# Self attention of a transformer decoder layer: units taken by threes, narrow diagonal blocks merged, max products placed one by one

## What is computed

```python
y = tgt                                   # (2, 2048, 512), 16 heads of 32
yn = _ln(y, dec_n1_s, dec_n1_b)
y = y + _mha(yn, yn, dec_sa_in_w, dec_sa_in_b, dec_sa_out_w, dec_sa_out_b, sb)   # sb: relative bias + causal mask
y = y + _mha(_ln(y, dec_n2_s, dec_n2_b), memory, dec_ca_in_w, dec_ca_in_b, dec_ca_out_w, dec_ca_out_b, cb)
h = _ln(y, dec_n3_s, dec_n3_b)
y = y + (jax.nn.relu(h @ dec_ff1_w.T + dec_ff1_b) @ dec_ff2_w.T + dec_ff2_b)
```

## Time and profile before

| | |
|---|---|
| median of 3 runs | 2791.2 us (2790.24 to 2792.56) |
| the profiled execution | 2795.43 us, its span 2793.4 us |
| mean granted TensorE clock | 0.987 |
| busy TensorE (PE), weight loads (PEld) | 2702.4 us (97%), 1791.0 us |
| busy VectorE (DVE), ScalarE (ACT) | 1583.1 us (57%), 1262.0 us (45%) |
| stage of self attention | from 396.8 us to 1600 us of the span |

### The profile page before, as it was taken

How to read it: one execution, slowest core, us unless ns; L and a number is a source line. 1 busy time by engine, 2 the same in 40 slices (tenths; PEclk the granted TensorE clock), 3 DMA queues, 4 the chain that set the end, 5 groups by cost and what they waited for, 6 DMA issues and landing times. The chain is left out here.

```text
span 2793.4 us, 40069 instructions
## 1 busy us (share of the span) xinstructions
PE 2702.4 (97%) x12704; PEld 1791.0 (64%) x12704; DVE 1583.1 (57%) x3827; ACT 1262.0 (45%) x2656; POOL 417.2 (15%) x497
## 2 busy tenths in 40 slices
PE   7999989999999999999999899999999999999998
PEld 6788854444444444444444378767778888888886
DVE  5554367777777777777777377567643222222211
ACT  2322113555555555555555545588833322332231
POOL 5000021000000000000000332188556000000000
PEclk9999988999999999999999999999999999999999
DMA  7656663222222222222222398555431000000000
GB/s 223 214 194 200 197 163 83 69 67 69 69 69 70 70 71 69 61 63 60 56 58 54 90 243 259 197 176 182 149 114 50 16 31 31 30 0 30 31 16 15
DMA packets 138950, 272.96 MB, mean 98 GB/s; under 512 B 24886, under 2 KB 56118, under 8 KB 133499
## 3 DMA queue, kind: packets, MB, share of 16 engines
q1 hardware_dynamic: 133530, 255.14, 31.7%
q0 software_dynamic: 5216, 15.33, 1.8%
HBM read 176.02 MB, written 99.98 MB: 99 GB/s over the span
## 5 line engine op out<-in xcount | busy, mean ns | idle before, releaser
L1302 ACT ACTIVATE sa_pr<-sa_st 128x512 f32<-128x512 f32 (+3 forms) x1280 | 611.0, 532 | 536.8 <-DVE sa_st L1365 293.8
L1268 PE MATMUL sa_ov<-sa_pr,sa_v 128*33 128x512 f32 (+3 forms) x2560 | 535.0, 539 | 0.0
L1349 DVE TENSOR_REDUCE sa_part<-sa_mp 128x1 f32<-128x512 f32 x760 | 408.3, 583 | 115.1 <-PE sa_mp L1247 114.3
L1257 PE MATMUL sa_st<-sa_q,sa_k 97*128 97x512 f32 (+3 forms) x1280 | 441.4, 413 | 17.9 <-ACT sa_pr L1302 13.5
L1257 PEld LDWEIGHTS sa_st<-sa_q,sa_k 97*128 97x128 f32 x1280 | 216.3, 189 | 319.7 <-ACT sa_pr L1302 213.0
L1247 PE MATMUL sa_mp<-sa_k,sa_q 96*128 96x512 f32 (+1 forms) x1256 | 362.0, 382 | 10.3 <-PEq L1229 5.3
L1346 DVE CUSTOM_DVE_ANT_0 sa_mp<-sa_mp,sa_ub 128x512 f32<-128x512 f32 (+1 forms) x496 | 308.4, 665 | 77.0 <-PE sa_mp L1247 72.9
L149 PE MATMUL ff_f<-sa_q,ff_w 128*128 128x512 f32 x1024 | 337.2, 390 | 3.1 <-PEq L2068 3.1
L2063 PE MATMUL ff_o<-ff_w,ca_q 128*128 128x512 f32 x1280 | 330.0, 392 | 3.7 <-DVE ca_q L2114 3.7
L2114 DVE TENSOR_TENSOR ca_q<-ca_v,ca_q 128x512 fp32r<-128x512 f32 x128 | 97.5, 762 | 379.3 <-ACT ca_q L2098 379.3
L1268 PEld LDWEIGHTS sa_ov<-sa_pr,sa_v 128*33 128x33 f32 x2560 | 122.0, 110 | 256.2 <-issue 206.6
(11 more groups left out here) (240 smaller groups left out, 3276.7 us busy)
## 6 DMA issues: line engine op xcount, KB each, us to landing
sa_q<-scratch_q SPq DMA_DIRECT2D x96, 256.0 KB, 7.7
sa_k<-scratch_k SPq DMA_DIRECT2D x96, 256.0 KB, 8.9
scratch_q<-sao_qst SPq DMA_DIRECT2D x32, 512.0 KB, 6.6
ca_q<-scratch_q SPq DMA_DIRECT2D x32, 512.0 KB, 4.6
scratch_q<-sa_q SPq DMA_DIRECT2D x28, 512.0 KB, 8.1
scratch_k<-sa_q SPq DMA_DIRECT2D x28, 512.0 KB, 5.3
sa_v<-scratch_v SPq DMA_DIRECT2D x16, 528.0 KB, 13.0
scratch_o<-sa_osb SPq DMA_DIRECT2D x128, 66.0 KB
```

The costliest lines, as they stand in the source:

```text
L1257: pe.matmul(st[bank(u, h)][:, 0:w], ks[n.par][:, h, kb * P:(kb + 1) * P], qs[n.par][:, h, g * GW + c0:(g + 1) * GW], start=True, stop=True ...
L1268: last = pe.matmul(ov[64 * h:64 * h + VW, c0:GW], vs[n.par][:, kb, h, :], pr[:, u % 4, h, 0:GW - c0], start=(u in opens), stop=(u in ends))
L1302: act.activation(pr[:, u % 4, h, 0:w], st[bank(u, h)][:, 0:w], ACT.Exp, scale=SCALE).then_inc(s["exp"], 1)
L1349: dve.tensor_reduce(to, tile, AX_X, ALU.max).then_inc(s["red"], 1)
```

## The change

What it does:

- **Merged blocks.** In each group the block that covers 128 columns and the block that covers 384 share one score tile of 512 columns for each head (unit "P", two matmuls into one tile), and the block that covers 256 columns holds both heads in one tile (unit "J"). "D" is the full-width diagonal block, "B" the last block before the diagonal, "F" any earlier one. Four units of eight tiles become three units of five tiles; a slot has 36 units and 68 tiles for ScalarE instead of 40 and 80. The matmuls are the same.
- **Batches of three** units (13 in a slot instead of 20, a few of them with two). `sa_pr` has six places instead of four.
- **Single max products.** A max product of one head is the smallest piece; four PSUM tiles of one bank take the place of two of two banks. Tables say how many go before each score tile (`MAX_BEFORE`, TensorE) and how many maxima before each bias addition (`REDUCED_BEFORE`, VectorE). The first product of the next slot stands at the start of batch 4 (counted from 0).
- **Opening tables** of its own for slot 0, with 10 products ahead of the first score instead of 4.
- **SyncE's order** in a usual slot: `store(n,0)`, `row(n,2)`, `load(n+1)`, `row(n,3)`, `store(n,1)`, `store(n,2)`, `row(n+1,0)`, `row(n+1,1)`, `store(n,3)`. The load gets one more DMA, 128 columns of the bias table that are there twice now. Slot 0 issues its load first.
- The sums and their inverses move into a buffer of cross attention that is idle at that time.

```diff
-SELF_ORDER = ((0, 2, 3, 1),
...
-STEPS_FROM = 12
...
+SELF_ORDER = ('DPJ', 'FFPFDJB', 'FFFFFBFJPFD', 'FFFFFJFFBFFDFFP')
+BATCHES = ((3,), (3, 2, 2), (3, 3, 3, 2), (3, 3, 3, 3, 3))
+SLOTS = 6
+MAX_FROM = 4
+OPENING_MAX = 35
+MAX_BEFORE = ((1, 0, 3, 1, 1, 1, 0), (1, 2, 0, 2, 1), (0, 0, 3, 1), (0, 1, 1, 0, 0, 0, 1), (2, 1, 2, 0, 2, 1, 1),
...
+REDUCED_BEFORE = ((6, 0, 1), (3, 0, 3), (0, 1, 0, 3), (3,), (9, 0, 0), (7, 0, 0, 1), (5, 0, 0), (7,), (8, 0),
...
+            elif kind == "P":
+                tiles = both(3 * P, 0, (d + 3, 3 * P, 0), (d + 1, P, P))
             else:
+                tiles = [Tile([Part(h, d + 2, 2 * P, 2 * P * h) for h in range(2)], 2 * P, P)]
...
-        tb = [k.sb(f"{name}_tb{i}", [P, 2, 2 * P]) for i in range(2)]
+        tb = [k.sb(f"{name}_tb{i}", [P, 2, 3 * P]) for i in range(2)]
-        pr = k.sb(f"{name}_pr", [P, 4, 2, GW])
+        pr = k.sb(f"{name}_pr", [P, SLOTS, 2, GW])
-        mp = [k.ps(f"{name}_mp{i}", [P, 2, GW]) for i in range(2)]
+        mp = [k.ps(f"{name}_mp{i}", [P, GW]) for i in range(NMB)]
...
             def slot(n, left):
...
+                else:
+                    store(n, 0)
+                    if left == 0:
+                        store_inverses()
+                    row(n, 2)
+                    if left >= 1:
+                        load(n + 1)
+                    row(n, 3)
+                    store(n, 1)
+                    if left == 0:
+                        load_second()
+                    store(n, 2)
+                    if left >= 1:
+                        row(n + 1, 0)
+                    if left >= 1:
+                        row(n + 1, 1)
+                    store(n, 3)
...
+            def max_product(n, x):
+                if x == 0:
                     landed(pe, n, "in", 6)
...
+                waits(pe, s["exp"], NTL * n + emptied(i) + 2)
+                for h, kb, c0, at in tile.parts:
+                    last = pe.matmul(st[i % NST][:, at:at + GW - c0], ks[n.par][:, h, kb * P:(kb + 1) * P],
+                                     qs[n.par][:, h, g * GW + c0:(g + 1) * GW], start=True, stop=True)
+                last.then_inc(s["scores"], 1)
...
             def slot(n, left):
-                for u in range(0, NU, 2):
-                    if isinstance(n.n, int) and n.n == 0 and u == 0:
+                for j in range(NJ):
+                    if is_first(n) and j == 0:
                         pe.wait_ge(s["init"], inits)
-                    ahead = list(after(n, u, left))
-                    for i in range(2):
-                        if ahead:
-                            scores(*ahead[i])
-                        for m, a in steps_at(n, u + i, left):
-                            max_step(m, a)
-                    values(n, u)
-                    values(n, u + 1)
+                    for maxima, ahead in places(n, left, (opening if is_first(n) else usual)[j], following(n, j, left)):
+                        for m, x in maxima:
+                            max_product(m, x)
+                        for m, i in ahead:
+                            scores(m, i)
+                    for u in batches[j]:
+                        values(n, u)
```

More of the change, by code:

```diff
@@ L930, in self_units @@
+OPENING_REDUCED_BEFORE = ((9, 0, 1), (5, 0, 2), (4, 0, 3, 0), (12,), (10, 2, 0), (9, 0, 0, 0), (8, 0, 1), (9,),
+                          (9, 1), (7, 0, 1), (5, 0, 3), (6, 0, 0), (0, 0, 4, 0, 0, 2))
+INVERSE_AT = 1
+Unit = namedtuple("Unit", "group tiles")
+Tile = namedtuple("Tile", "parts biased table")
+Part = namedtuple("Part", "head block first at")
 def self_units():
+    both = lambda biased, table, *blocks: [Tile([Part(h, *x) for x in blocks], biased, table) for h in range(2)]
     out = []
@@ L941, in self_units, with self_batches @@
+        assert next(far, None) is None and sum(BATCHES[g]) == len(order)
+    return out
+def self_batches():
+    out, u = [], 0
+    for size in itertools.chain(*BATCHES):
+        out.append(range(u, u + size))
+        u += size
     return out
@@ L1049, in self_attention @@
     N = NPAIR * B
[L1050 to L1058, removed]
@@ L1059, in self_attention @@
-    NCH = 1 + max(m[3] for m in msteps if m is not TURN)
-    usual, opening = self_steps_at(NU, NM)
+    units, batches, products = self_units(), self_batches(), self_max_products()
+    NU, NJ, NX = len(units), len(batches), len(products)
+    opens = [min(u for u in range(NU) if units[u].group == g) for g in range(GB)]
+    ends = {max(u for u in range(NU) if units[u].group == g): g for g in range(GB)}
+    tiles = [(u, t) for u in range(NU) for t in units[u].tiles]
+    tiles_of = [[i for i, (v, _) in enumerate(tiles) if v == u] for u in range(NU)]
@@ new lines, in self_attention @@
+    near = [i for i, (_, t) in enumerate(tiles) if t.biased]
+    NTL, NB = len(tiles), len(near)
+    turns = [x for x in range(NX) if products[x] is TURN]
+    heads_of_max = [x for x in range(NX) if x not in turns]
+    late = next(x for x in heads_of_max if products[x][0] >= KB // 2)
+    last_of = [max(x for x in heads_of_max if products[x][0] // TT == g) for g in range(GB)]
+    NCH = 1 + max(products[x][3] for x in heads_of_max)
+    begun = sum(sum(MAX_BEFORE[j]) for j in range(MAX_FROM, NJ))
@@ L1064, in self_attention, with emptied @@
     ROW = (3 * HD, 3 * HD)
[L1066 to L1086, removed]
+    def emptied(i):
+        return i - NST if i >= NST else max(e for e in range(NTL) if e % NST == i) - NTL
@@ new lines, in following, with places, is_first, width @@
+    def following(n, j, left):
+        if j + 1 < NJ:
+            return [(n, i) for u in batches[j + 1] for i in tiles_of[u]]
+        return [(n + 1, i) for u in batches[0] for i in tiles_of[u]] if left else []
+    def places(n, left, places_of, ahead):
+        for i, places_here in enumerate(places_of):
+            yield [(n + d if d else n, x) for d, x in places_here if left >= d], ahead[i:i + 1]
+    def is_first(n):
+        return isinstance(n.n, int) and n.n == 0
+    def width(i):
+        return sum(GW - p.first for p in tiles[i][1].parts)
```

299 lines of the change are left out of this document (154 added, 145 removed), and 3 rows, old and new, of the table SELF_ORDER.

## The result

| | before | after |
|---|---|---|
| median | 2791.2 us (2790.24 to 2795.99) | **2775.0 us** (2773.57 to 2782.22) |
| ratio | | 0.9943, 95% interval 0.9927 to 0.9958 |
| the profiled execution | 2795.43 us, span 2793.4 | 2773.57 us, span 2771.5 |
| mean granted TensorE clock | 0.987 | 0.977 |

A forecast was written before the change was run, and what follows sets the result against it. TensorE was taken as the bound, paying about 0.3 us a batch for changing matmul kind, plus waits. Usual slots −3.5, slot 15 −2 and slot 0 −6 made −11.5 off 2791.2: 2780 us, range 2712 to 2812.

The forecast's parts named there:

- The load decides: Usual slots: the load, queued behind store(n,0), lands at about 22.0 us; TensorE idles about 3.5 us at batch 4.
- The clock: Usual slots: after the idle TensorE falls to 1.2 GHz, costing 1.7 us a slot, ends 0 and 3.4.
- load in time: Rival, usual slots: the load lands before TensorE needs it; slot 68.1 us, total 2710 us; chance 0.14.
- my own prices: Usual slot: 62.3 us of matmuls the change does not touch, about 0.3 us a batch for changing matmul kind, plus waits.
- VectorE: Usual slots: busy 55.2 us instead of 57.2, off the path; waits of sa_mp over 3 us would make the forecast wrong.
- Usual slots together: Fourteen usual slots at 73.1 us against 73.35: fourteen times −0.25 is −3.5 us.
- Slot 0: First slot: early load and even table remove half of the low-clock losses, −6 us, ends −12 and +5.
- Slot 15: Last slot: loads nothing and has fewer batches, −2 us.
- loads nothing: −2.1 by its batches: Step for the last slot: no load there, so only the fewer batches count, −2.1, taken as −2 us.
- The sum: Whole kernel: −3.5 − 2 − 6 = −11.5 us off the median 2791.2, giving 2780 us.
- The forecast of the likeliest case: Whole kernel: late load stalls TensorE and the clock falls in usual slots; 2780 us, own range 2762 to 2800, chance 0.42.

The follow-up runs named there:

- Experiment 1: Changed kernel with row(n,2) and the next slot's load issued before store(n,0) in usual slots: 2712.1 us, ratio 0.9708 to the kernel before.
- experiment 2: Changed kernel with 11 additional unused matmuls ahead of the product that waits for the load: 2756.2 us, ratio 0.9873 to the kernel before.
- experiments 8 to 10: Version of experiment 5 with 16 batches: 2781.4 us; that with maxima moved: 2760.0 us; version of experiment 5 with merging and threes undone, 20 batches: 2900.1 us.
- experiment 5: Changed kernel with the load ahead of store(n,0) in usual slots and row(n,2) ahead of store(n,0) and the inverses in the last: 2699.7 us.
- Experiment 6: Kernel before with one table altered, max steps spread evenly over the units of slot 0: 2782.2 us, ratio 0.9959.
- Experiment 4: Changed kernel with row(n,2) ahead of store_inverses in the last slot alone: 2767.1 us, ratio 0.9908 to the kernel before.
- experiment 3: Changed kernel with 5 additional unused matmuls ahead of the product that waits for the load: 2762.4 us, ratio 0.9901 to the kernel before.
- experiment 8: Version of experiment 5 with 16 batches in a slot instead of 13, products and maxima in the same order: 2781.4 us, ratio 0.9951.

## Why the prediction was right, and where it was not

**The load decides.** Right, and nearly to the number. Predicted: issued 9.4 us after batch 0 began, landed 12.8 us later, batch 4 reached at 18.2 to 18.6, idle 3.5. Measured: issued 8.1 us after, landed 12.8 us later (570.63 to 583.39), idle 2.7 on average, inside the ends 1 and 4.5. What I had too long was the way to the load: I added up 5.3 for the batch and 4.1 for the copy, stores and rows. The batch took 5.4 and the rest 2.7. Batch 4 was reached after 18.5 us, as said. Experiment 1 shows the cause.

**The clock.** Predicted 1.7 us a slot, the shortest stretch; measured 2.0 in batch 4, and 1.7 by experiment 2. Twelve of fourteen stalls were followed by a fall. The Trainium skill, "TensorE: Matmul & The Clock Gate", section "HAM oscillation — how this bites in real kernels", says that a loop that waits for a DMA in each turn pays in each turn; the trace agrees in those twelve, while the two idles of 2.14 and 2.16 us passed. The example in that section of the Trainium skill has waits of about 3 to 5 us; here waits of 2.17 to 3.96 us were enough.

**The slot without the stall.** The rival "load in time" gave it 68.1 us; experiment 1 measures 68.4. Without the fall at slot 8 it is 68.0. So a gain of 5 us a slot was in the changed kernel all along. My split of it stays unproven. By my own prices the slot is 62.3 + 3.9 + 2.2 = 68.4, with waits of 2.2 where I said 1.9, and the 5 us are 2.1 of fixed cost and 2.8 of waits; one could as well put them down as seven batches at 0.7. No run changes the number of batches alone: experiments 8 to 10 bring jams of their own.

**VectorE.** Waits for it of over 3 us would have spoken against the forecast. TensorE's max products waited for VectorE 0.2 us in all of the usual slots. Their weight loads, which overlap other matmuls, did so for 42 us (22 in the kernel before), but in the version of experiment 5, where it is 51, the slot is at its shortest.

**Usual slots together.** −6.3 us instead of −3.5. The errors were −0.8 (idle), +0.3 (clock) and +0.3 (the slot without a stall: 67.9 in my sum, and 72.9 − 2.7 − 2.0 = 68.2), 73.1 to 72.9 in all.

**Slot 0** was mis-sized: −15.2 where I said −6, beyond its better end of −12. I took half of the losses of clock as gone; in the stretch 395.9 to 450.5 the clock rose from 0.69 to 0.83, and TensorE did 196 matmuls instead of 126 there. Experiment 6 shows 10 of the 15.

**Slot 15** has the wrong sign: +4.6 where I said −2. The step that failed is "loads nothing: −2.1 by its batches". I followed the load past the store and the row in the new queue of the usual slots and left out the same queue in the last slot, where `store_inverses` now stands ahead of `row(n,2)`, not only of `row(n,3)`. Experiment 4 shows it: 8 us by the medians, and a slot 15 of 60.4 us, 5.2 under the kernel before.

**The sum.** −11.5 predicted, −16.2 in the medians. In the spans of the two profiled executions it is −21.9: the sum with its three errors (−9.2 in slot 0, −2.8 in the usual slots, +6.6 in slot 15) makes −16.9, and −5.0 lie outside the stage; the profiled execution before was 4.2 above its median and the one after 1.5 below. The forecast of the likeliest case held with its mechanism; that the total came so near is partly luck, since the misses in slot 0 and slot 15, each larger than the whole error of the total, offset each other.

## What to carry to other kernels

When a load is moved within a queue, add up what now stands ahead of it until its landing, and set that against the work ahead of its first user: here 20.9 against 18.5 us (slot 2) undid most of a gain of 5 us a slot, and the cure was three lines in the order of one queue. Do that sum for the first and the last turn of the loop too, where other entries stand in the same queue. And tables that interleave two engines by counts belong to the batches they were made for; regrouped unchanged, with three more batches, they made the kernel 3% slower.

## What the runs showed of the hardware that was not expected

An idle of TensorE of 1.22 us in an otherwise dense stage was followed by granted clock 0.5 (experiment 3), and in experiment 8 two of 0.63 and 0.60 us within one batch were. Idles of 2.14, 2.16 and 2.23 us passed in the changed kernel, and one of 2.83 in that of experiment 4. So the length of one idle does not decide over this range. Behind a stall, a fall costs 1.4 us at the least and 4.2 at the most in batch 4. Matmuls of no use, 2.6 us of them a slot, bought back 19 us of the whole.

The time that the sixth q or k DMA needs to land hardly depends on where in the slot the load stands: over fourteen loads the median is 8.5 us before, 8.3 in the changed kernel and 8.3 in experiment 1, all between 7.4 and 9.3 (the 9.3 of the earlier trace rows was the longest). The share of the DMA engines is 1.00 to 1.05 while the load of the changed kernel runs (the stretches 576.60 to 590.20). An earlier start was one way to have it in time; asking for its data later, or another order within the load, was not tried.
